# A decoder layer in split fp32: two head-output splits moved between the exps

## Time and profile before

| | |
|---|---|
| median of 3 runs | 955.51 us (953.96 to 957.34) |
| profiled execution | 957.34 us |
| its span, first to last instruction | 955.5 us |
| mean granted TensorE clock | 0.993 |
| attention part | from the first scores at 24.0 us to about 652 us |
| a step with j=4 or 5 | 8.16 to 8.2 us |
| a step with j=0 to 3 | 9.55 us |

### The profile page before, as it was taken

The page is one execution under the profiler, slowest core; times in us unless marked ns, Lnnn a source line. Parts: engine busy times, 40 slices in busy tenths (PEclk is TensorE's granted clock), DMA queues, the critical chain, the costliest instruction groups (busy, mean ns, idle before and its releaser), DMA issues. The chain is left out here.

```text
span 955.5 us, 18425 instructions
## 1 busy us (share of the span) xinstructions
PE 933.3 (98%) x6242; PEld 800.8 (84%) x6242; DVE 647.5 (68%) x1758; ACT 539.0 (56%) x1731; POOL 231.6 (24%) x243
## 2 busy tenths in 40 slices
PE   7999999999999999999999999998899999999998
PEld 6788889889888878988888888886788888888887
DVE  5788788787788777767767767775843553553453
ACT  3877677677768777867776777786401400400400
POOL 0443124124214434512422432434100000000000
PEclk8999999999999999999999999999999999999999
DMA  7300000000001020000000020112000000000000
GB/s 215 116 24 2 1 1 0 0 0 0 0 0 45 23 67 2 1 23 0 0 22 0 0 88 0 46 45 89 23 12 12 0 11 11 0 11 11 1 12 11
DMA packets 13184, 22.07 MB, mean 23 GB/s; under 512 B 1108, under 2 KB 7764, under 8 KB 12628
## 3 DMA queue, kind: packets, MB, share of 16 engines
q1 hardware_dynamic: 13140, 21.51, 6.8%
HBM read 19.41 MB, written 2.10 MB: 23 GB/s over the span
## 5 line engine op out<-in xcount | busy, mean ns | idle before, releaser
L383 POOL TENSOR_TENSOR prob<-prob,rsum 128x512 f32<-128x512 f32 x128 | 133.2, 1040 | 399.3 <-DVE rsum L580 399.3
L462 ACT ACTIVATE prob<-psS,nmin 128x128 f32<-128x128 f32 x512 | 181.0, 377 | 7.8 <-DVE nmin L564 4.4
L549 DVE TENSOR_TENSOR oT_lo<-psT,oT_hi 64x256 fp32r<-64x256 f32 x256 | 107.9, 422 | 12.8 <-ACT oT_hi L450 2.9
L444 ACT ACTIVATE pT_hi<-psT 128x512 fp32r<-128x512 f32 x128 | 69.6, 595 | 77.4 <-PE psT L721 77.4
L462 ACT ACTIVATION_READ_ACCUMULATOR prob<-psS,nmin 128x1 f32 x512 | 111.8, 218 | 0.0
L450 ACT ACTIVATE oT_hi<-psT 64x256 fp32r<-64x256 f32 x256 | 96.9, 379 | 7.9 <-PE psT L124 3.3
L542 DVE TENSOR_TENSOR pT_lo<-psT,pT_hi 128x512 fp32r<-128x512 f32 x128 | 82.2, 682 | 0.9 <-ACT pT_hi L444 0.8
L122 PE MATMUL psT<-pT_lo,v_hi 128*128 128x256 f32 x256 | 73.7, 288 | 6.1 <-DVE pT_lo L542 6.1
L536 DVE TENSOR_TENSOR v_lo<-psW,v_hi 128x512 fp32r<-128x512 f32 x64 | 44.1, 690 | 44.6 <-ACT v_hi L439 44.6
L709 PE MATMUL psS<-kt_lo,q_hi 64*128 64x128 f32 x512 | 73.7, 285 | 0.0
L124 PE MATMUL psT<-pT_hi,v_lo 128*128 128x256 f32 x256 | 73.0, 285 | 0.0
(11 more groups left out here) (196 smaller groups left out, 2574.0 us busy)
## 6 DMA issues: line engine op xcount, KB each, us to landing
stage<-w SPq DMA_DIRECT2D x4, 1024.0 KB, 4.8
stage<-ctxT SPq DMA_DIRECT2D x4, 512.0 KB, 4.2
out<-fin SPq DMA_DIRECT2D x16, 128.0 KB, 1.7
xres<-x SPq DMA_DIRECT2D x3, 512.0 KB, 8.4
stage<-wq SPq DMA_DIRECT2D x2, 512.0 KB, 5.9
stage<-wk SPq DMA_DIRECT2D x2, 512.0 KB, 6.1
stage<-wv SPq DMA_DIRECT2D x2, 512.0 KB, 5.9
stage<-wr SPq DMA_DIRECT2D x2, 512.0 KB, 4.9
```

Of the source, the lines that this page charges most:

```text
L383: nc.gpsimd.tensor_tensor(prob[:, r, :], prob[:, r, :], rsum[:, r].unsqueeze(2).broadcast_to([P, TPG, P]), ALU.mult).then_inc(prob_done, 1)
L444: nc.scalar.activation(pT[0][:, i, :], psT[:, i, :], ACT.Copy).then_inc(pT_hi, 1)
L462: e = nc.scalar.activation(prob[:, n, :], flat(psS[:])[:, n * P:(n + 1) * P], ACT.Exp, bias=nmin[:, n:n + 1], scale=-1.0, accum_out=psums[ ...
L549: nc.vector.tensor_tensor(oT[1][r, parity, b, :], banks(psT)[r, b, h, :], oT[0][r, parity, b, :].bitcast(F32), ALU.subtract).then_inc(oT_l ...
```

## The change

`oT_split` is taken into the loop over the two halves, on ScalarE and on VectorE alike. ScalarE's order becomes: exps of half 0, q and k copies (and the context's), oT copies of half 0, exps of half 1, oT copies of half 1. VectorE's becomes: reciprocal 0, q_lo and kt_lo, oT_lo of half 0, reciprocal 1, oT_lo of half 1. Waits, counts and operands stay as they are. The first step, which has no oT, and the last two halves behind the loops are untouched.

```diff
--- before.py
+++ after.py
@@ -466,8 +466,7 @@
                             qk_split(G, j + 1)
                             if j == PAIRS - 2 and after == 1:
                                 split_context(G + 1 - NGRP)
-                    if not first:
-                        for i in range(2):
+                        if not first:
                             oT_split(s, (j + 1) % 2, i)
                     if j < TPG:
                         v_split(G, 1, j, 0)
```

## The result

The changed kernel takes **962.42 us** (median of 6 runs, 961.47 to 964.17), the kernel before 955.92 in the same series (953.26 to 957.78): ratio 1.0078, 95% interval 1.0063 to 1.0093. It is slower by 6.5 us; the interval holds 6.0 to 8.9. (The ratio is not the quotient of these two medians: the record lists 15 executions of the changed kernel for it, whose median is 962.87.) The forecast was 964, with a range of 959 to 969. The profiled execution took 962.98 us, its span is 961.2, the mean granted clock 0.996.

A forecast was written before the change was run, and what follows sets the result against it. TensorE, busy 98% of the span, bounds the kernel. Losses of 4.9+0.6+1.75+0.45+0.65=8.35 us on the median 955.51 gave 963.9, forecast 964 us, range 959 to 969.

The forecast's parts named there:

- steps 28 to 30: Weight-swap steps: later oT copies delay weight pieces and pT_lo, handing on +1.75 us in all; bounds 0.4 and 2.5.
- the end: Step 63: the last four transposes start at 644.95 instead of 644.33, +0.65 us, with nothing following to hide them.
- Slack 0.77 against shift 1.04, 14 bare steps: Steps j=4, 5 without 28, 29: second exps shift 1.04 us against 0.77 slack, 0.35 lost each, 4.9 in all.
- The pickup: TensorE's delay in starting after its releaser: 0.04 us at the quickest, 0.15 at the most.
- Cover in j=0 to 3, 7, and 6 without context: Work ahead of the next scores (v_project, v_first_half, z transposes) covers the 1.04 us shift: cost nothing.
- Context steps: j=6 in G=4 to 6, where ScalarE also splits the context: 0.2 us each, three steps, 0.6 in all.
- Both ends: Step 1: next scores later, +0.45 us; step 63: last four transposes later, +0.65 us.
- VectorE and GpSimd at nothing: Every step: subtractions fill VectorE's idle time, and GpSimd's later multiply still has some 0.6 us of cover: no cost.
- The exps do not come in time: Answers the rival that exps stay in time at the 14 steps and the three: at most 2.85 us, 958.4; chance 0.11.
- an earlier oT_lo: Rival: VectorE reaches weight pieces and pT_lo earlier, taking away up to 6.4 us of TensorE's waits: 949.1; chance 0.05.
- The clock did not fall for the short stalls: Answers the rival that TensorE's clock halves behind step 30's gap (966) or also behind 14 short stalls (980); chance 0.09.

The follow-up runs named there:

- two copies without the wait: Changed kernel, with half 0's oT copies between the second and third exp of half 1, so weighted_values is done by then: 957.19 us against 955.08, ratio 1.0020.
- the wait without the copies: Kernel before, with ScalarE's wait for the first half of weighted_values put ahead of the exps of half 1, no copy moved: 962.03 us, ratio 1.0069.
- the kernel with the swaps apart: Kernel before, with the upper halves of weights xq and xk converted one step later (ends of steps 33 and 34): 952.71 us against 955.08, ratio 0.9975.
- the kernel that changes only covered steps: Kernel before, with the change only in 36 steps (j=0 to 3 without step 1; j=6, 7 of groups 0 to 2): 956.84 us against 955.55, ratio 1.0016.
- ScalarE's half alone: Kernel before with only ScalarE's part of the change, VectorE in its old order: 978.06 us, ratio 1.0233.
- VectorE's part alone: Kernel before with only VectorE's part of the change, ScalarE in its old order: 958.64 us, ratio 1.0032.

## Why the prediction was right, point by point

The mechanism came as forecast, and most terms of the sum with it. That the sum is so near (8.35 for 8.12) is in part luck: steps 28 to 30, the end, step 62 and the steps without a term are off by -0.49, +0.29, -0.62 and +0.73 us, which nearly cancel.

**Slack 0.77 against shift 1.04, 14 bare steps.** Right: 4.85 us for 4.9. The experiments show both ends of it: steps with cover shift by as much and cost next to nothing, two copies without the wait cost 0.08 in most steps, the wait without the copies 0. The pickup was 0.05 us (465.88 to 465.93), at the quick end; in steps 1, 28, 29, 60 and 61 it was 0.15.

**Cover in j=0 to 3, 7, and 6 without context.** Right in the main. Steps 7, 15 and 23 pay 0.12 each, 33 0.13, and 10, 18, 26 up to 0.1; "nothing" was a little too good, and why it is these steps was not taken apart.

**Context steps.** Right, 0.16 each for 0.2. Its last accumulator read and the next scores, as the earlier trace rows:

```profile
481.27 0.77 ACT L450 ACTIVATE oT_hi<-psT 64x256 fp32r<-64x256 f32 x2
...
483.35 0.21 ACT L462 ACTIVATION_READ_ACCUMULATOR prob<-psS,nmin 128x1 f32 x1
```

```profile
483.62 0.33 PE L707 MATMUL psS<-kt_lo,q_hi 64*128 64x128 f32 x2
```

The copies follow the context copy without a wait, as the step's working said.

**Steps 28 to 30.** Mechanism right; against the profiled execution of the kernel before, the size is 0.5 us too large: 1.26 for 1.75. TensorE, then VectorE of the changed kernel, as the earlier trace rows:

```profile
302.76 0.33 PE L707 MATMUL psS<-kt_lo,q_hi 64*128 64x128 f32 x2 [0.36 <-ACT prob L462]
...
309.03 0.36 PE L122 MATMUL psT<-pT_lo,v_hi 128*128 128x256 f32 x1 [0.89 <-DVE pT_lo L541]
...
312.47 0.33 PE L707 MATMUL psS<-kt_lo,q_hi 64*128 64x128 f32 x2 [0.36 <-ACT prob L462]
...
318.65 0.38 PE L122 MATMUL psT<-pT_lo,v_hi 128*128 128x256 f32 x1 [0.80 <-DVE pT_lo L541]
```

```profile
304.38 1.23 DVE L252 SCALAR_TENSOR_TENSOR wk_lo<-stage,wk_hi 128x1024 fp32r<-128x1024 f32 x1 [0.61 <-ACT wk_hi L248]
...
314.09 1.23 DVE L252 SCALAR_TENSOR_TENSOR wv_lo<-stage,wv_hi 128x1024 fp32r<-128x1024 f32 x1 [0.61 <-ACT wv_hi L248]
```

Steps 28 and 29 came as worked out (+0.44 and +0.83). Step 30 should have handed on another 0.5 through a later wv_lo. wv_lo was later, but took 1.23 us instead of the 1.69 that it had taken before; the prediction had moved the instruction and kept its duration. TensorE's gap in step 30 is 0.80, not 1.29.

But the 1.69 is not this kernel's fixed value. Up to step 31 the kernel with the swaps apart is the kernel before, and there wv_lo takes 1.23. VectorE and GpSimd in step 30, first of the kernel before, then of that one:

```profile
311.75 1.69 DVE L252 SCALAR_TENSOR_TENSOR wv_lo<-stage,wv_hi 128x1024 fp32r<-128x1024 f32 x1 [0.51 <-ACT wv_hi L248]
```

```profile
311.74 2.17 POOL L165 TENSOR_TENSOR z<-z,rstd 128x256 f32<-128x256 f32 x2
```

```profile
308.84 1.23 DVE L252 SCALAR_TENSOR_TENSOR wv_lo<-stage,wv_hi 128x1024 fp32r<-128x1024 f32 x1 [0.51 <-ACT wv_hi L248]
```

```profile
308.84 2.27 POOL L165 TENSOR_TENSOR z<-z,rstd 128x256 f32<-128x256 f32 x2
```

Step 30 lasts 10.11 us in the first and 9.66 in the second (9.65 in the kernel that changes only covered steps). Against 9.66 the changed kernel's 10.10 is 0.44 longer, close to the 0.5 of the forecast, and the three steps together lose 1.7 us. So some 0.45 us of the difference between forecast and table are scatter of the one execution that the table is taken from.

Step 62 is 0.62 us *shorter*, which the prediction didn't have, and this is not scatter: w_lo took 1.67 there in all three of those traces. Now it takes 1.23, and starts 0.18 us earlier in the step, as step 61 grew by more than the piece was delayed.

**Both ends.** Step 1 right (0.47 for 0.45). Step 63 lost 0.94 instead of 0.65, as in this trace weighted_values itself starts 0.32 later in the step (4.47 after its scores instead of 4.15): 

```profile
645.22 0.39 PE L122 MATMUL psT<-pT_lo,v_hi 128*128 128x256 f32 x1 [0.49 <-DVE pT_lo L541]
...
649.93 0.66 PE L719 MATMUL psT<-ident,prob 128*128 128x128 f32 x4 [1.17 <-POOL prob L383]
```

Step 62 ends earlier while ScalarE and VectorE do not, so VectorE's z_lo, minima and pT_lo reach further into step 63. The bracket of the last row names GpSimd's multiply as worked out.

**VectorE and GpSimd at nothing.** Right for the change as made, but the reason was too thin: VectorE's half isn't neutral, it saves what ScalarE's half would cost there (962 against 978).

**The rivals.** The exps do not come in time (new line in the waits). The change as a whole gained nothing by an earlier oT_lo; what that is worth shows only against ScalarE's half alone (962 against 978). The clock did not fall for the short stalls: in stretches of 3 us from 36 to 655 us the changed kernel's granted clock is 1.00 everywhere except for the 6 us behind the gap of 2.4 us in step 33. The rule of the Trainium skill on TensorE's idleness ("TensorE: Matmul & The Clock Gate", Part 1) thus found nothing to act on in the 17 waits of at most 0.4 us. Taking away the one gap of 2.4 us took its slow stretch away, but the gap does not always bring one. In the kernel with ScalarE's part alone TensorE waits the same 2.38 us in step 33, up to 364.10, and these are the 3 us behind it, to set beside the earlier trace rows:

```profile
364.00:367.00 3.00, 2.90 (x24) 2.93 (x25) 1.33 (x3) 2.52 (x11) 1.04 (x1) 1.00 0.22 85
```

The clock stays at 1.00, its 2.4 GHz level, and the step lasts 12.15 us instead of 13.54: the slow stretch was worth 1.4 us. What decides between the two is open here.

**Size by the medians.** 8.1 us by the traces against 6.5 by the medians, both inside the measured interval of 6.0 to 8.9.

## What to carry to other kernels

Before work is moved ahead of an instruction that another engine waits for, compare its whole shift, the moved work plus the wait that it brings along, with the slack at the place with the least cover, and multiply by the number of such places: here 1.03 us against 0.77, fourteen times. A wait that fits the slack at all those places can still close a ring where another chain is tight already, and then cost as much as the change itself. Move the partner's half along: the engine behind the one that comes late should have its ready work ahead of its own wait.

## What was unexpected of the hardware

A subtraction of a weight piece on VectorE (1024 elements a partition) takes 1.23 us in some places and up to 1.69 in others. It took 1.66 to 1.69 where GpSimd's multiplication of z had started 0.01 to 0.03 us ahead of it. From the kernel before, at the turn from step 61 to 62, on VectorE and on GpSimd, and then from the changed kernel:

```profile
627.94 1.67 DVE L252 SCALAR_TENSOR_TENSOR w_lo<-stage,w_hi 128x1024 fp32r<-128x1024 f32 x1 [0.52 <-ACT w_hi L248]
```

```profile
627.91 2.17 POOL L165 TENSOR_TENSOR z<-z,rstd 128x256 f32<-128x256 f32 x2
```

```profile
633.04 1.23 DVE L252 SCALAR_TENSOR_TENSOR w_lo<-stage,w_hi 128x1024 fp32r<-128x1024 f32 x1 [0.61 <-ACT w_hi L248]
```

```profile
632.55 2.19 POOL L161 TENSOR_TENSOR z<-xres,mv 128x256 f32<-128x256 f32 x2
...
634.82 1.19 POOL L165 TENSOR_TENSOR z<-z,rstd 128x256 f32<-128x256 f32 x2
```

Before, the two start 0.03 us apart and both are slow (GpSimd's pair 2.17 instead of 1.19). After, GpSimd's earlier pair is under way for 0.5 us when VectorE starts; VectorE then has its full speed and GpSimd alone pays (2.19 for the pair that took 1.18 before). The wait-only kernel shows the reverse move: its wk_lo starts 0.03 us behind GpSimd's multiplication and takes 1.66 where it had taken 1.23. With GpSimd 0.13 us ahead (VectorE's part alone, step 30) VectorE takes 1.56. In the same hundredth (step 29 of the kernel before, both at 302.93, and step 30 of the kernel with the swaps apart) VectorE keeps 1.23 and GpSimd's pair takes 2.27.

These durations add up as if one of the two had to finish its instruction before the other's could go on: GpSimd's pair is two instructions of about 0.6 us, and VectorE loses 0.44 when the first has just begun, 0.33 when it began 0.13 earlier and nothing at 0.5; GpSimd's pair loses 1.0 to 1.1 us each time (2.17 to 2.27 for 1.19). That is worked out from the rows and was not tested by an experiment of its own. A shift of some tenths on one engine, or the scatter of a hundredth, can so change durations on two engines, in either direction.
